# First round of a graph kernel: additions between the two comparisons of a group, block numbers loaded word by word

## The chip, the cores and the metric

The kernel runs on one core of a Trainium2 chip. The metric is the device time of one execution in microseconds (us); lower is better. Engines are named as the profile names them: PE is TensorE, PEld its weight loads, DVE VectorE, ACT ScalarE, POOL GpSimd, SP SyncE.

## The reference, cut to what matters

There are 12500 nodes with 64 features and 400000 edges `(src, dst)`, sorted by `dst`. Three rounds each sum rows of a node table over the edges that end in a node (`segment_sum`); between them stand small products, a relu and two layer norms.

```python
def _L0_gnn_ref(x, src, dst, W_fc, b_fc, W_res, b_res):
    agg = jax.ops.segment_sum(x[src], dst, num_segments=n)
    deg = jax.ops.segment_sum(jnp.ones_like(dst, dtype=x.dtype), dst, num_segments=n)
    mean = agg / jnp.maximum(deg, 1.0)[:, None]
    h = jnp.concatenate([x, mean], axis=-1) @ W_fc + b_fc
    h = jax.nn.relu(h)
    return h + x @ W_res + b_res
...
def _general_conv(x, edge_attr, src, dst, Wm, bm, We, be, Ws, bs):
    msg = x[src] @ Wm + bm + edge_attr @ We + be
    agg = jax.ops.segment_sum(msg, dst, num_segments=x.shape[0])
    return agg + x @ Ws + bs
...
x = _layernorm(x + _L0_gnn_ref(x, src, dst, ...), axis=-1)
x = _layernorm(x + _L1_gnn_ref(x, edge_index, edge_attr_64, ...), axis=-1)
```

## The kernel before

**The first round**, which the change touches, fills about 260 to 1485 us of the span. It goes over 72 blocks of 128 destination nodes, two per turn of a loop (`j` is 0 or 1); the work on one block is called a half here. For each block it builds a 128 x 12544 matrix of edge counts and multiplies it with the node table. The edges are cut into steps of 128. For a step VectorE writes two comparisons into a ring of 16 places (`hot_c`): the high one, which marks the source block and the place in a window of `wd` destination nodes, and the low one, which marks the source lane (both by `pairs`, whose instruction is line 816). TensorE multiplies the one with the other (L1149), ScalarE copies the counts out of PSUM (L1418), SyncE stores them, and TensorE multiplies the counts of the block before with the table (the dense product, L1126, in 16 pieces of 6 or 7 matmuls).

**Widths.** Windows are 1 node wide in blocks 0 to 7, 2 nodes in blocks 8 to 29, 4 nodes in blocks 30 to 71. So a half has 128 steps at width one (after the first two blocks, which have several steps for a window), 64 at width two and 32 at width four. The comparisons come in groups: 8 steps (`many`) at widths one and two, 4 at width four. A half thus has 16, 8 and 8 groups. Width two holds 22 halves, 486 to 860 us; width four 42 halves, from 858 us.

**The handshake.** Before a group VectorE waits on `stepped`, which lets it start when TensorE has done the steps of the group two before (8-step groups; 4-step groups have four places in the ring). The low comparison of a group raises `made`, on which TensorE waits before the steps of the group.

**Edges that are not counted in the matrix** are gathered: GpSimd issues 7 indirect DMAs for a half (L1288), VectorE marks their destination lanes (`hot_g`, L797), TensorE multiplies them at the end of the half (L1118, 21 matmuls) into 7 sums. VectorE then adds, in the next half, with one instruction each:

- part 0: the reduction of the dense product into `part_d` (L853), after waits on `b_used` and `gsum`, and before it the load of 7 block numbers, packed in two words, into registers (`load_blocks`, whose instruction is L471)
- part 1: `part_d` to its block of `acc` (L859)
- parts 2 to 8: the 7 sums, each to a block of `acc` that a loaded number names (L865); each waits on `s_add`, which the addition before it raises
- part 9: a semaphore (`gred`).

Part `n` stands at window 10 + 2n of the half. At width one each such window begins a group; at widths two and four every second one does (windows 12, 16, 20, 24, 28), and the others (10, 14, 18, 22, 26) lie within one. Where a group begins, the order is: wait on `stepped`, high comparison, low comparison, then the part.

The order on each engine is the order in the code; nothing reorders it.

## Time and profile before

| what | value |
|---|---|
| median of 3 runs (lowest, highest) | 3532.28 us (3532.06, 3535.52) |
| the profiled execution | 3533.11 us, span 3531.3 us |
| PE busy | 3093.6 us, 88% |
| DVE busy | 2388.2 us, 68% |
| POOL busy | 2120.9 us, 60% |
| ACT busy | 1585.1 us, 45% |
| L816, comparisons of the first round | x1384, 911.7 us busy |
| L865, additions of gathered sums | x504, 110.0 us busy, 69.0 us idle before them |
| L853, reductions of the first round | x72 |

The profile is one execution. A group of instructions is given with its count, busy time and the time its engine sat idle in front of it. A busy PE counts modelled ends of pipelined matmuls, so its rate is better read from the distance between starts.

### The profile page before, as it was taken

The numbers are of one execution on the slowest core, as the hardware profiler recorded it, in microseconds if no ns is written. First come the engines' busy times: TensorE is split into PE (matmuls) and PEld (weight loads), VectorE is DVE, ScalarE is ACT, GpSimd is POOL, SyncE is SP. The second block draws the span as 40 slices with busy tenths as digits, with TensorE's granted clock in tenths as the row PEclk, the third lists the DMA queues.
The fourth block names the chain that finished last, engine by engine and source line by source line (L and its number), as shares of the span: only waits on it lengthen the run. The fifth ranks groups of instructions, "written<-read, shape, count | busy, mean of one in ns | idle before, by whom it ended". The sixth has DMA issues, their size and how long they took to land.

```text
span 3531.3 us, 114817 instructions
## 1 busy us (share of the span) xinstructions
PE 3093.6 (88%) x38568; PEld 2874.1 (81%) x38568; DVE 2388.2 (68%) x6286; ACT 1585.1 (45%) x2164; POOL 2120.9 (60%) x2436
## 2 busy tenths in 40 slices
PE   0128999999999999899999979999999889999995
PEld 0127988888888888788888879999999789999995
DVE  8679998888888888799999673333333433333335
ACT  0122677778999999789999550000000400000000
POOL 5771345455666666544444257777777777777774
PEclk9859999999999999999999879999999999999998
DMA  3521455556666666678888439999999499999995
GB/s 87 144 19 44 163 196 208 202 211 229 239 244 243 244 242 243 233 229 253 253 253 252 119 139 384 393 396 381 400 384 384 172 363 394 393 387 398 386 388 222
DMA packets 234014, 928.09 MB, mean 263 GB/s; under 512 B 46723, under 2 KB 146193, under 8 KB 178030
## 3 DMA queue, kind: packets, MB, share of 16 engines
q1 hardware_dynamic: 182405, 844.73, 63.8%
q0 software_dynamic: 51392, 80.97, 7.9%
q10 hardware_dynamic: 154, 1.60, 0.2%
q8 instruction: 34, 0.56, 0.1%
q14 instruction: 29, 0.24, 0.0%
HBM read 676.56 MB, written 250.56 MB: 263 GB/s over the span
## 4 chain that ended last, share of the span: by engine, by line
PE 40%; POOL 19%; issue 17%; DVE 14%; DMA 5%; DVEq 5%; ACT 1%; ACTq 0%; POOLq 0%; SPq 0%
PE ps L1126 27%; POOL msg L1288 13%; PE ps L1149 8%; DVE union L816 5%; DMA msg<-y_tab,idx 3%; POOL abuf L1230 3%; DVE union L931 3%; PE ps L1118 3%; DVE abuf L944 3%; DVEq L944 2%; DVEq L471 2%; POOL union L1230 1%; PE ps L1086 1%; DMA abuf<-in_x_dram 1%; PE ps L1205 1%
## 5 line engine op out<-in xcount | busy, mean ns | idle before, releaser
L1288 POOL DMA_INDIRECT msg<-y_tab,idx x1512 | 1611.3, 1066 | 922.2 <-issue 469.6
L1126 PE MATMUL ps<-union,abuf 128*128 128x192 bf16 x14112 | 1206.4, 248 | 14.9 <-DVEq L787 10.2
L1126 PEld LDWEIGHTS ps<-union,abuf 128*128 128x128 f16 x14112 | 1173.6, 99 | 17.9 <-issue 10.6
L1418 ACT ACTIVATE abuf<-ps 128x784 f16<-128x784 f32 x1152 | 949.1, 824 | 261.4 <-PE ps L1149 236.6
L816 DVE TENSOR_TENSOR union<-lane,union 128x1568 f16<-128x1568 f16 (+1 forms) x1384 | 911.7, 710 | 8.5 <-PE ps L1149 4.6
L1126 PE MATMUL ps<-early,abuf 128*128 128x195 bf16 x7154 | 809.3, 249 | 0.0
L1126 PEld LDWEIGHTS ps<-early,abuf 128*128 128x128 f16 x7154 | 641.9, 99 | 92.1
L1149 PE MATMUL ps<-union 128*128 128x98 f16 (+2 forms) x4192 | 661.8, 287 | 56.7 <-DVE union L816 55.5
L1394 ACT ACTIVATE idx<-src_g 128x7 int32 (+1 forms) x216 | 44.4, 205 | 1257.1 <-PE ps L1118 1237.9
L808 DVE TENSOR_TENSOR acc<-acc,ps 128x64 f32 (+1 forms) x1015 | 225.0, 222 | 412.4 <-DVE acc L808 239.3
L1196 PE MATMUL ps<-union 128*64 128x128 f32 x7280 | 458.7, 278 | 24.0 <-ACT union L1440 19.6
L1196 PEld LDWEIGHTS ps<-union 128*64 128x64 f32 x7280 | 395.5, 137 | 87.4 <-DVE abuf L944 74.3
L1440 ACT ACTIVATE union<-union 128x1280 f32<-128x1280 f16 x364 | 443.5, 1268 | 35.8 <-DVE union L931 35.3
L1149 PEld LDWEIGHTS ps<-union 128*128 128x128 f16 x4192 | 353.7, 108 | 98.5 <-issue 59.3
L1308 POOL TENSOR_TENSOR rel_e<-early,base_e 128x10 f16 x728 | 226.1, 330 | 247.4 <-DVE union L931 244.5
L931 DVE TENSOR_TENSOR union<-lane,rel_e 128x640 f16<-128x640 f16 x728 | 352.2, 484 | 4.4 <-POOL rel_e L1308 1.4
L895 DVE TENSOR_REDUCE part_d<-ps 128x64 f32<-128x192 f32 x144 | 51.6, 358 | 353.1 <-PE ps L1126 353.1
L794 DVE TENSOR_SCALAR hot_g<-lane,codes 128x128 f16<-128x128 f16 x1008 | 184.2, 269 | 63.9 <-DVE acc L808 62.2
L1118 PE MATMUL ps<-msg,hot_g 128*128 128x64 bf16 (+1 forms) x4536 | 181.7, 195 | 45.8 <-DMA msg<-y_tab,idx 45.3
L944 DVE TENSOR_TENSOR abuf<-abuf,ps 128x128 f32 x728 | 204.9, 281 | 15.8 <-issue 7.2
L1118 PEld LDWEIGHTS ps<-msg,hot_g 128*128 128x128 f16 x4536 | 169.1, 99 | 54.4 <-DMA msg<-y_tab,idx 53.8
L865 DVE TENSOR_TENSOR acc<-acc,ps 128x65 f32 x504 | 110.0, 218 | 69.0 <-DVE acc L865 53.8
(229 smaller groups left out, 1342.2 us busy)
## 6 DMA issues: line engine op xcount, KB each, us to landing
abuf<-a_dram SPq DMA_DIRECT2D x288, 1568.0 KB
a_dram<-abuf SPq DMA_DIRECT2D x72, 3136.0 KB
union<-in_edge_attr_dram SPq DMA_DIRECT2D x728, 160.0 KB, 3.1
msg<-y_tab,idx POOLq DMA_INDIRECT x1512
y_tab<-union SPq DMA_DIRECT2D x28, 336.0 KB, 2.2
abuf<-in_x_dram SPq DMA_DIRECT2D x28, 224.0 KB, 3.5
y_tab<-early SPq DMA_DIRECT2D x7, 682.5 KB, 5.2
out_dram<-union SPq DMA_DIRECT2D x2, 800.0 KB, 3.5
```

Source lines behind the costliest of these rows:

```text
L808: V.tensor_tensor(to, to, tile_ps(r, j, k).unsqueeze(1), ALU.add).then_inc(s_add[r], 1)
L816: return V.tensor_tensor(to.rearrange("p s (c u) -> p s c u", u=2), lanes.unsqueeze(1).to_broadcast([P, n, width // 2, 2]), codes[:, which ...
L931: marks = V.tensor_tensor(mark_e[:, h, :, :].rearrange("p j (c u) -> p j c u", u=2), lane16[:, 0:P].rearrange("p (c u) -> p c u", u=2).uns ...
L944: V.tensor_tensor(to, to, ps[:, b, 0:P], ALU.add).then_inc(e_add, 1)
L1118: last = nc.tensor.matmul(tile_ps(r, j, k), hot_g[:, s, :], msg[:, s, c * width_of[r]:(c + 1) * width_of[r]], start=c == 0, stop=c == 2)
L1126: last = nc.tensor.matmul(ps[:, bank, 0:3 * width_of[r]], abuf[:, buffer, hi * P:(hi + 1) * P], ycols[r][:, hi, :], start=hi == 0, stop=hi ...
L1149: nc.tensor.matmul(ps[:, w % 4, 0:WIN].rearrange("p (h d) -> p h d", d=WD)[:, :, d0:d0 + wd], hot_c[:, n, WIN:WIN + P], hot_c[:, n, 0:HIS ...
L1196: last = nc.tensor.matmul(ps[half:half + D, h, 0:P], feats[:, h, j * D:(j + 1) * D], hot_e[:, h, j, :], start=j < 2, stop=j >= EG - 2)
L1288: pool.indirect_dma_start(msg[:, s, 0:3 * width_of[r]], None, y_tab[r], bass.IndirectOffsetOnAxis(ap=idx[:, s:s + 1], axis=0)).then_inc(ga ...
L1308: nc.gpsimd.tensor_tensor(rel_e[:, h, :, :], flat(dst_e[:, bass.ds(grp[h], 1), :]).unsqueeze(2) .to_broadcast([P, EG, 2]), base_e[:, bass. ...
L1418: A.activation(abuf[:, j, :].rearrange("p (h w d) -> p w h d", w=WPB, d=WD) [:, w:w + 2, :, :], ps[:, w % 4:w % 4 + 2, 0:WIN].rearrange("p ...
L1440: A.activation(hot_e[:, h:h + 2, :, :], mark_e[:, h:h + 2, :, :], ACT.Copy)\
```

## The change

`load_blocks` is called twice with 4 numbers (one word) instead of once with 8 (two words): at window 6 and at window 8 of the half, no longer behind the wait on `b_used` at window 10. The parts are put into a function `beside`, which is called behind the high comparison and ahead of the low one where a window begins a group. Where it does not, the part stands where it stood. Each part has the same waits as before.

```diff
+                        gathers, words = b0 < 2 * GI, []
+                        def beside(window, it, j, i):
+                            part, odd = divmod(window - 10, 2)
+                            if odd or part < -2 or part > (G + 2 if gathers else 1):
+                                return
+                            before = it * (2 * (G + 1)) + (1 + j * (G + 1))
+                            if part < 0:
+                                if gathers:
+                                    words.extend(load_blocks((it * 2 + j) * (GW // 4) + (part + 2), 4))
+                            elif part == 0:
+                                dve.wait_ge(b_used[j], it + (1 + j))
+                                if gathers:
+                                    dve.wait_ge(gsum[0][1 - j], it + (1 + j))
+                                V.tensor_reduce(part_d[:, j, :], ...).then_inc(b_red[j], 1)
...
+                                dve.wait_ge(s_add[0], before + (k + 1))
+                                if k < G:
+                                    to = flat(acc[:, bass.ds(words[-GW + k], 1), :])
+                                    V.tensor_tensor(to, to, tile_ps(0, 1 - j, k), ALU.add).then_inc(s_add[0], 1)
...
                                         dve.wait_ge(stepped, i * pair + (q + e0 + many - HB + 1))
                                         pairs(hot_c[:, n:n + many, 0:HIS * wd], twice_h, s, HIS * wd)
+                                    if q in upto[j]:
+                                        beside(upto[j].index(q), it, j, i)
+                                    if q % many == 0:
                                         pairs(hot_c[:, n:n + many, WIN:WIN + P], twice_l, s, P).then_inc(made, many // HB)
-                                    if q not in upto[j]:
-                                        continue
...
-                                            bs = load_blocks((it * 2 + j) * (GW // 4), GW)
```

On VectorE at width two, around the loads and the reduction. ISA and REGISTER_ALU rows set registers; 128x8x196 is a high comparison, 128x8x128 a low one. Before:

```order
L816 ISA [waits stepped]
L816 TENSOR_TENSOR union<-lane,union 128x8x196
L816 ISA
L816 TENSOR_TENSOR union<-lane,union 128x8x128
L471 ISA [waits b_used0]
L471 TENSOR_LOAD steps
L853 TENSOR_REDUCE part_d<-ps 128x65 [waits gsum0_1]
```

And now:

```order
L471 ISA
L471 TENSOR_LOAD steps
L868 REGISTER_ALU
L816 ISA [waits stepped]
L816 TENSOR_TENSOR union<-lane,union 128x8x196
L471 ISA
L471 TENSOR_LOAD steps
L816 ISA
L816 TENSOR_TENSOR union<-lane,union 128x8x128
L844 TENSOR_REDUCE part_d<-ps 128x65 [waits gsum0_1,b_used0]
```

The first load stands a group earlier, the second between the two comparisons of the last group ahead of the reduction.

On VectorE at width two, one group with two additions (`acc<-acc,ps`). Before:

```order
L816 TENSOR_TENSOR union<-lane,union 128x8x196
L816 ISA
L816 TENSOR_TENSOR union<-lane,union 128x8x128
L862 REGISTER_ALU
L865 ISA [waits s_add0]
L865 TENSOR_TENSOR acc<-acc,ps 128x65
L862 REGISTER_ALU
L865 REGISTER_ALU [waits s_add0]
L865 ISA
L865 TENSOR_TENSOR acc<-acc,ps 128x65
```

And now:

```order
L816 TENSOR_TENSOR union<-lane,union 128x8x196
L852 REGISTER_ALU
L855 ISA [waits s_add0]
L855 TENSOR_TENSOR acc<-acc,ps 128x65
L816 ISA
L816 TENSOR_TENSOR union<-lane,union 128x8x128
L852 REGISTER_ALU
L855 REGISTER_ALU [waits s_add0]
L855 ISA
L855 TENSOR_TENSOR acc<-acc,ps 128x65
```

The two additions no longer follow each other: the low comparison stands between them.

On VectorE at width one, the load. Before:

```order
L816 ISA [waits stepped]
L816 TENSOR_TENSOR union<-lane,union 128x8x98
L816 ISA
L816 TENSOR_TENSOR union<-lane,union 128x8x128
L471 ISA [waits b_used0]
L471 TENSOR_LOAD steps
L853 TENSOR_REDUCE part_d<-ps 128x65 [waits gsum0_1]
```

And now:

```order
L816 TENSOR_TENSOR union<-lane,union 128x8x98
L471 ISA
L471 TENSOR_LOAD steps
L816 ISA
L816 TENSOR_TENSOR union<-lane,union 128x8x128
L868 REGISTER_ALU
L816 ISA [waits stepped]
L816 TENSOR_TENSOR union<-lane,union 128x8x98
L471 ISA
L471 TENSOR_LOAD steps
L816 ISA
L816 TENSOR_TENSOR union<-lane,union 128x8x128
```

Both loads stand between the comparisons of a group here. The order on PE, ACT, POOL and SP is the same in both kernels.

## Rows read from the trace of the kernel before

**Rows 1.** Widths two, four: busy us PE, PEld, DVE, ACT, POOL; clock, DMA share, GB/s
```profile
486.00:860.00 374.00, 340.48 (x4062) 315.22 (x4060) 335.29 (x576) 292.87 (x377) 191.22 (x154) 1.00 0.55 210
860.00:1000.00 140.00, 137.56 (x1426) 115.58 (x1425) 124.03 (x252) 125.89 (x161) 93.74 (x68) 1.00 0.65 249
```

**Rows 2.** Waits at width two, 488 to 860 us: total us, times, longest
```profile
PEld ps L1149 <- issue: 58.7, 111, 0.6
PE ps L1149 <- DVE union L816: 33.5, 111, 0.4
DVE acc L865 <- DVE acc L865: 18.5, 66, 0.3
DVE part_d L853 <- issue: 10.5, 22, 0.5
```

**Rows 3.** Timeline of DVE at width two: start, us, instruction, idle before it
```profile
506.44 1.58 DVE L816 TENSOR_TENSOR union<-lane,union 128x1568 f16<-128x1568 f16 x2 [0.16 <-PE ps L1149]
508.51 0.36 DVE L853 TENSOR_REDUCE part_d<-ps 128x65 f32<-128x195 f32 x1 [0.49 <-issue]
508.79 1.57 DVE L816 TENSOR_TENSOR union<-lane,union 128x1568 f16<-128x1568 f16 x2
...
510.97 1.58 DVE L816 TENSOR_TENSOR union<-lane,union 128x1568 f16<-128x1568 f16 x2
512.46 0.21 DVE L865 TENSOR_TENSOR acc<-acc,ps 128x65 f32 x1
512.98 0.22 DVE L865 TENSOR_TENSOR acc<-acc,ps 128x65 f32 x1 [0.30 <-DVE acc L865]
513.22 1.58 DVE L816 TENSOR_TENSOR union<-lane,union 128x1568 f16<-128x1568 f16 x2
```

**Rows 4.** Timeline of PE in the same half
```profile
504.24 0.84 PE L1118 MATMUL ps<-msg,hot_g 128*128 128x65 bf16 x21
504.92 0.51 PE L1149 MATMUL ps<-union 128*128 128x196 f16 x4
...
506.64 0.50 PE L1149 MATMUL ps<-union 128*128 128x196 f16 x4
...
510.49 0.51 PE L1149 MATMUL ps<-union 128*128 128x196 f16 x4 [0.27 <-DVE union L816]
...
521.85 0.51 PE L1149 MATMUL ps<-union 128*128 128x196 f16 x4
```

**Rows 5.** Timeline of DVE at width one
```profile
411.97 0.21 DVE L865 TENSOR_TENSOR acc<-acc,ps 128x65 f32 x1
412.10 1.15 DVE L816 TENSOR_TENSOR union<-lane,union 128x784 f16<-128x784 f16 x2
```

**Rows 6.** Loads of block numbers (L471), four stretches: ns shortest/median/longest; the last: one word each
```profile
L471 DVEq TENSOR_LOAD <-steps x6: 1796/1843/1912, 364.7 to 471.3; - x6
L471 DVEq TENSOR_LOAD <-steps x23: 525/1722/1775, 489.8 to 859.4; - x23
L471 DVEq TENSOR_LOAD <-steps x42: 524/528/533, 873.8 to 1471.2; - x42
L471 DVEq TENSOR_LOAD <-steps x183: 299/305/526, 1501.6 to 1975.9; - x183
```

**Rows 7.** Timeline at width four, two of POOL's gathers and one pair of DVE
```profile
1009.74 1.31 DVE L816 TENSOR_TENSOR union<-lane,union 128x1568 f16<-128x1568 f16 x2
1009.92 1.62 POOL L1288 DMA_INDIRECT msg<-y_tab,idx  x1 [0.30 <-issue]
...
1019.04 0.94 POOL L1288 DMA_INDIRECT msg<-y_tab,idx  x1 [0.30 <-issue]
```

**Rows 8.** Wait for gathers at width four, 860 to 1485 us: total us, times, longest
```profile
PEld ps L1118 <- DMA msg<-y_tab,idx: 12.2, 21, 1.5
```

**Rows 9.** Timeline of POOL at width two: the first gather of the half
```profile
505.76 1.34 POOL L1288 DMA_INDIRECT msg<-y_tab,idx  x1 [7.06 <-ACT idx L1394]
```

**Rows 10.** Chain of waits at width four: start, us; from the last gather's start until it landed
```profile
1019.04 2.58 DMA msg<-y_tab,idx
```

34 lines of the change are left out of this document (10 added, 24 removed).

## The prediction

> **What bounds the kernel now.** First the busy time by stretch: the change touches only the first round, so the question is what ends last at each width. At width four PE is busy 137.6 of 140 us and DVE 124.0; at width two PE has 340.5 of 374 and DVE 335.3. The granted clock is 1.00 in both [rows 1]. So width four is TensorE's, and width two is shared: neither engine is full, which means that they wait for each other.
>
> The waits at width two say where. PE waits 111 times for comparisons, five times in each of 22 halves; its matmuls show 33.5 us and its weight loads 58.7 us [rows 2]. DVE waits 66 times for its own last addition, 18.5 us, and 22 times with nothing to wait for but its queue in front of the reduction, 10.5 us [rows 2].
>
> The timeline of one half shows the mechanism. A pair of comparisons that begins at 510.97 makes room for an addition at 512.46, 1.49 us later. The next addition needs the semaphore of the first, sits idle for 0.30 us and starts at 512.98, and the next pair starts at 513.22: 0.76 us for two additions, 2.25 us for the group [rows 3]. TensorE, undisturbed, starts at 504.92 and is two of its pieces of 4 steps (with their dense matmuls) further at 506.64: 1.72 us for a group of 8 steps [rows 4]. So while there are additions VectorE needs 2.25 us for what TensorE does in 1.72, and ring places are only two groups. From 504.92 to 521.85 the half takes 16.93 us. TensorE's own work in it is 8 x 1.715, plus 0.17 for the two pieces with a seventh dense matmul, plus 0.68 for the gathered product (504.24 to 504.92): 14.57 us [rows 4]. The difference, 2.36 us, times 22 is 52 us, and agrees with the 58.7 us of the weight loads: this is the most that width two can give.
>
> **The change part by part.**
>
> *Additions apart.* Where an addition follows and precedes comparisons and its semaphore has long come, as at width one, it costs the distance from 411.97 to 412.10: 0.13 us, since it overlaps with both neighbours [rows 5]. With a comparison between any two additions I take that price for both: the group costs 1.49 + 0.26 = 1.75 us instead of 2.25. The bounds are 0.13 and the 0.38 of each of two dependent additions (0.76 / 2) [rows 3, 5]; I take the low one because the waited-for addition is then at least one low comparison old.
>
> *What it costs in `made`.* The low comparison now ends behind an addition, so a group takes 1.57 + 0.13 = 1.70 us from its start to `made`. I walk through the half with three distances. The high comparison starts at the earliest 1.52 us after TensorE starts the group two before (504.92 to 506.44); TensorE starts 0.13 us after the pair ends (508.79 + 1.57 = 510.36, to 510.49); TensorE needs 1.715 us for a group [rows 3, 4]. Zero is 504.92. Group 2 starts at 1.52 as before, the reduction 1.49 later at 3.01 and group 3 another 0.28 later, at 3.29 (before: 3.87). Its steps start at 3.29 + 1.70 + 0.13 = 5.12, and TensorE is free for them at 5.15. Group 4: 5.04, steps at 6.87 (free at 6.87). Then VectorE starts every 1.75 us: 6.79, 8.54, 10.29, and TensorE starts at 8.62, 10.37 and, since group 7 has no addition, 12.09. From there 1.715 + 0.17 + 0.68 gives 14.65 us for the half. The waits are almost gone, and the bound is TensorE again.
>
> *Loads.* Before, the load of two words stood bare in front of the reduction: 0.49 us of idle at width two [rows 3]. It is in front of the reduction no more. The load at window 6 stands behind a finished pair, ahead of a wait for TensorE at 1.52, and is hidden by that wait. The load at window 8 stands between the comparisons of group 2. What one word costs there no row shows. The ends are 0.305 us, the median of single words in the later edge stage, and 1.91 us, the longest load of two words at width one; in this very stage two words took 1.72 us, but 0.53 at width four [rows 6]. I take half of 1.72, 0.86 us. About 0.9 us of the high comparison cover it (it has 1568 of the pair's 2592 elements, so 0.6 of 1.49 us), and with the register work ahead of it the low comparison is some 0.2 us late. That moves groups 3 to 7 by 0.2: 14.85 us for the half; I take 14.8. So 16.93 - 14.8 = 2.1 us, times 22 = **46 us** gained. With 0.305 us for the word it is 50 us.
>
> *Width one* (6 halves): each part already stood between two groups, so there was no idle to win. One load of 1.84 us behind a pair of 1.15 goes, of which some 1.0 was bare [rows 5, 6]; two loads behind a high comparison of about 0.55, half of a pair, come. At 0.86 each, and with register work, they stick out by about 0.5 each: nothing gained, nothing lost. Ends: -6 us (both hidden) and, at 1.84 us a word, 2 x 1.5 - 1.0 = 2.0 us a half, +12. The blocks before 362 us have the same order in two halves more: 0, at most 4 us lost.
>
> *Width four* (42 halves): the additions win the same 0.5 us a group on VectorE, and it is waste, since TensorE is full. What is late there is the gather: TensorE waits in every second half for the last of 7 gathers, 21 times, 12.2 us in all [rows 8]. A gather takes 0.94 us at its shortest. The one at 1009.92 lasts until 1011.54, 0.49 us past the end (1011.05) of the pair that was started just before it [rows 7], and the next begins 0.30 later, 1.92 us after the first. A group with two additions is 1.31 - 0.09 + 0.76 = 1.98 us here at most, so gathers seem to go in step with the groups, and such a group becomes 1.22 + 0.26 = 1.48. Some five gathers in step win 0.4 us each, more than the wait. I take **10 us**. Ends: 0 and 12.2 us.
>
> The Trainium skill (SBUF — State Buffer, section Who interferes with whom) says that a VectorE instruction with two SBUF inputs blocks a GpSimd instruction that reads SBUF until it ends. The trace agrees as far as it goes: the gather that began 0.18 us after a pair lasts 1.62 us, the shortest 0.94 [rows 7]. Were it a slowdown by share of time instead, denser comparisons would make gathers slower, and the 10 us would not come.
>
> *Clock, stores, evacuations*: at width two the DMA share would rise from 0.55 towards the 0.65 of width four, ACT's load from 292.9 / 374 to the level of 125.9 / 140 [rows 1]. Both are met there at the full clock, so I price them at nothing.
>
> Sum: 46 + 0 + 10 = 56 us from the profiled execution's 3533.1: 3477. The median of the runs lies 0.8 us below that execution; I say **3477 us**.
>
> **The rivals.**
>
> *The word costs as much as two did.* At 1.72 us the low comparison of group 2 comes 1.1 us late; the half becomes 15.7, 22 x 1.25 = 27 us. Width one loses 12, width four gives 10: 3508 us. For it: at widths one and two, where VectorE waits for TensorE, the typical load took 1.7 to 1.9 us [rows 6], and the second load keeps a place just behind such a wait. Against: the edge stage's words at 0.305.
>
> *The gathers become the bound.* The first one starts 1.52 us after the gathered product of the half before (504.24 to 505.76), six distances later the last one starts, and it lands 2.58 us on [rows 4, 9, 10]. In step with groups of 1.75 us that is 4.1 + 10.5 = 14.6 us: just the half. If they fall into a beat of 2.0 us, as at width four now, it is 4.1 + 12 = 16.1 us a half: 22 x 0.8 = 18 us and nothing at width four, 3515 us.
>
> *The gap stays.* The Trainium skill (VectorE: DVE Perf Modes, section The DRAIN you can't avoid) says that chained instructions cost the same with or without a semaphore after each, because the pipe drains anyway. As a mechanism here: the 0.76 us of two additions would be their own price wherever they stand, `made` would come later by it, and the load would be as long between the comparisons as it was bare. Then nothing changes: 3530 us. Against it stand 0.13 us at width one and 0.76 / 2 = 0.38 at width two for the same instruction [rows 3, 5].
>
> *Slower.* An addition between a high and a low comparison may lose its overlap on both sides and hold the low one, as a dependent addition does: (0.76 - 0.26) = 0.5 us more, now once a group ahead of `made`. Let x be that extra. Width two loses 4x in 22 halves (88x) of its 46; width one, where nothing was won, has 9 such additions in 6 halves (54x); width four has at least 1.6 us of room in a half (DVE's 16 idle us of 140 [rows 1]) and loses nothing at this x, but also wins nothing if gathers stay. At x = 0.5: -46 + 44 + 27 = +25, less 10 if the gathers still gain: +15, so 3548 us. It decides from x = 0.39, where 142x is 56. Against it: addition and comparison overlap today in both orders.
>
> **How the numbers follow.** Forecast 0.60, own range 3465 to 3492. Full price of a word 0.14; gathers bound 0.08; gap stays 0.05; slower 0.08; a gain beyond the forecast, with width one at its full speed, 0.05. A measurement tells about 0.2% (7 us) from no change. Faster by more: 0.60 + 0.14 + 0.08 + 0.05 = 0.87. Same 0.05. Slower 0.08. The range goes from 3463 (46 + 4 + 12 + 6 with nothing lost) to 3512, which takes in the full price of the word and nearly the gathers.
>
> **What would show it.** In the profile after, at width two: no idle time between additions; two pieces of TensorE every 1.72 us through the half; halves of 14.8 us; the 111 waits for L816 at under 15 us. The length of the single load between comparisons: 0.3, 0.9 or 1.7 us. At width four the waits for gathers gone, halves at 14.4, and the reduction waiting longer for the gathered product. Width one unchanged at 21 us a half. Wrong it would be if a low comparison starts more than 0.3 us behind the addition ahead of it, or gathers lie 1.9 us apart.

## The result and the profile after

The changed kernel takes **3624.8 us** (median of 4 runs, 3621.8 to 3627.1) against 3533.9 us for the kernel before: ratio 1.0256, 95% interval 1.024 to 1.0272. The forecast was 3477 us with a range from 3463 to 3512. It was wrong in sign: a gain was forecast and a loss came. One run of a later kernel (e6, 3758.5 us at a granted clock of 0.83) was in a slower state and is left out of every number.

The profiled execution took 3621.8 us, its span is 3620.0 us, 88.7 us longer than before. It splits at one instruction, the last `hot_g` of the first round, the last start in this row of the view of one line (duration ns, first and last start):

```profile
L797 DVE TENSOR_TENSOR hot_g<-code_g,lane x72: 1081/1084/1093, 260.3 to 1457.0; 128x896 f16<-128x896 f16 x72
```

```profile
L797 DVE TENSOR_TENSOR hot_g<-code_g,lane x72: 1082/1084/1093, 260.2 to 1525.1; 128x896 f16<-128x896 f16 x72
```

The first is the kernel before, the second the one after: 68.1 us are lost in the first round, and 20.6 us behind it. In what follows "last `hot_g`" is this number; it measures the first round alone. The first `hot_g` starts between 259.5 and 262.0 us in these kernels, so a difference of 2 us in it says nothing.

The table of stretches after, to be held against [rows 1]:

```profile
486.00:860.00 374.00, 290.62 (x3368) 280.15 (x3366) 264.50 (x476) 242.65 (x313) 191.92 (x128) 0.88 0.46 175
860.00:1000.00 140.00, 121.42 (x1330) 109.70 (x1330) 110.62 (x216) 106.18 (x137) 77.26 (x56) 0.93 0.54 204
1000.00:1480.00 480.00, 479.34 (x5012) 406.04 (x5011) 424.51 (x867) 441.25 (x565) 292.84 (x234) 1.00 0.66 247
```

From 486 to 860 us TensorE now does 3368 matmuls instead of 4062, every engine is less busy, and the granted clock is 0.88. From 1000 us on TensorE is full and the clock 1.00. So something stops all engines at width two. The waits between 488 and 1000 us name it:

```profile
ACT abuf L1423 <- PE ps L1154: 150.5, 61, 12.0
DVE union L816 <- PE ps L1154: 131.3, 32, 12.3
PEld ps L1123 <- DMA msg<-y_tab,idx: 104.3, 12, 10.6
PE ps L1154 <- DVE union L816: 0.3, 1, 0.3
```

The 111 waits of TensorE for comparisons [rows 2] are one of 0.3 us: the change did what it was for. In their place TensorE waits 12 times for the gathers (L1123 is the gathered product, L1118 before), up to 10.6 us, and ScalarE and VectorE wait for TensorE.

The timelines of VectorE, GpSimd, SyncE and TensorE around the first of these stops. In VectorE's, a row of 1568 elements with x2 is a high and a low comparison, one behind the other, and x4 is two such pairs:

```profile
498.41 0.22 DVE L855 TENSOR_TENSOR acc<-acc,ps 128x65 f32 x1
498.54 1.57 DVE L816 TENSOR_TENSOR union<-lane,union 128x1568 f16<-128x1568 f16 x2
500.03 1.09 DVE L797 TENSOR_TENSOR hot_g<-code_g,lane 128x896 f16<-128x896 f16 x1
501.03 3.06 DVE L816 TENSOR_TENSOR union<-lane,union 128x1568 f16<-128x1568 f16 x4
```

```profile
495.38 1.45 POOL L1293 DMA_INDIRECT msg<-y_tab,idx  x1 [0.30 <-issue]
497.14 1.44 POOL L1293 DMA_INDIRECT msg<-y_tab,idx  x1 [0.31 <-issue]
498.88 6.03 POOL L1293 DMA_INDIRECT msg<-y_tab,idx  x1 [0.30 <-issue]
505.21 0.94 POOL L1293 DMA_INDIRECT msg<-y_tab,idx  x1 [0.30 <-issue]
```

```profile
503.01 0.37 SPq L1554 DMA_DIRECT2D a_dram<-abuf  x1
```

```profile
511.04 1.33 PE L1123 MATMUL ps<-msg,hot_g 128*128 128x65 bf16 x21 [8.75 <-DMA msg<-y_tab,idx]
```

Read them together. The seventh gather of the half starts at 498.88, 0.34 us into the high comparison of the last group. It lasts 6.03 us; its neighbour behind it 0.94. It ends at 504.91, and VectorE's run without an idle moment ends at 501.03 + 3.06 = 504.09: 0.82 us earlier. Meanwhile SyncE has issued the half's 3.2 MB store at 503.01. TensorE gets the gathered rows only at 511.04. The 6 us gather comes 11 times, at 498.88, 539.55, 580.55 and so on to 908.30, in every second half: after a stop the next seven gathers run at 1.25 us apart on an idle VectorE, so the next half is not touched. At 662.53 it is the sixth gather of its half instead of the seventh: there GpSimd pauses for 1.76 us between its first and its second gather, where 0.30 us is usual. Each trace has such a pause of 1.7 to 1.8 us between 600 and 660 us, the kernel before too, and it is behind most of what the table below calls "once" or "all but one".

The stop costs TensorE its clock as well:

```profile
504.00:505.00 1.00, 0.00 (x0) 0.00 (x0) 0.09 (x1) 0.00 (x0) 0.91 (x1) 1.00 1.05 439
506.00:508.00 2.00, 0.00 (x0) 0.00 (x0) 0.00 (x0) 0.00 (x0) 1.39 (x3) 0.50 1.00 401
512.00:514.00 2.00, 2.00 (x19) 1.85 (x17) 0.00 (x0) 0.82 (x1) 1.33 (x2) 0.50 0.49 125
516.00:518.00 2.00, 2.00 (x24) 1.97 (x23) 1.32 (x3) 1.54 (x2) 0.00 (x0) 0.94 0.03 8
```

TensorE is idle from about 502.3 us; in the row from 506 on the granted clock is 0.50, the 1.2 GHz level, and it is still 0.50 for the first pieces behind the stop. Rows of the timeline of TensorE:

```profile
512.19 0.84 PE L1154 MATMUL ps<-union 128*128 128x196 f16 x4
...
513.81 0.86 PE L1154 MATMUL ps<-union 128*128 128x196 f16 x4
...
515.44 0.86 PE L1154 MATMUL ps<-union 128*128 128x196 f16 x4
...
516.69 0.50 PE L1154 MATMUL ps<-union 128*128 128x196 f16 x4
```

From the gathered product (511.04) to the first piece it is 1.15 us instead of 0.69, and the pieces are 1.62, 1.63 and 1.25 us apart instead of the 0.86 of the pieces from 516.69 on: 2.4 us lost in all. The row of 506 to 508 also shows the DMA engines full, at 401 GB/s; at that rate the 3.2 MB of the store take 8 us (an estimate from this row), from 503.4 to about 511.4, and TensorE gets the gathered rows at about that time.

The halves between the stops are as forecast: from one `hot_g` (525.85) to the next (540.70) 14.85 us; the forecast said 14.85 by its walk. The long halves take 25.8 to 26.8 us. So width two took 450.2 us instead of 371.8 (+78.4); blocks 30 to 71 took 589.6 instead of 599.9 (-10.3); width one and the blocks before it are unchanged (block 8 begins at 485.3 in both).

### The profile page after: what moved, and what is told of

The parts are those of the page before. It is cut to its first block, busy times and chain, and to the rows that moved or that the text cites. A ratio compares the mean times of both kernels' runs of the same rounds, so it can differ in the third digit from the quotient of the medians.

```text
span 3620.0 us, 115031 instructions
## 1 busy us (share of the span) xinstructions
PE 3125.4 (86%) x38568; PEld 2913.9 (80%) x38568; DVE 2370.9 (65%) x6286; ACT 1588.8 (44%) x2164; POOL 2123.0 (59%) x2436
## 4 chain that ended last, share of the span: by engine, by line
PE 45%; POOL 18%; issue 15%; DVE 10%; DMA 8%; DVEq 4%; ACT 1%; POOLq 0%; ACTq 0%; SPq 0%
PE ps L1131 30%; POOL msg L1293 12%; PE ps L1154 10%; DMA msg<-y_tab,idx 6%; POOL abuf L1235 3%; DVE union L936 3%; PE ps L1123 3%; DVE abuf L949 2%; DVE union L816 2%; DVEq L949 2%; DVEq L471 1%; POOL union L1235 1%; PE ps L1210 1%; PE ps L1091 1%; DMA abuf<-in_x_dram 1%
## 5 line engine op out<-in xcount | busy, mean ns | idle before, releaser
L1131 PEld LDWEIGHTS ps<-union,abuf 128*128 128x128 f16 x14112 | 1173.1, 99 | 16.7 <-issue 10.6
L816 DVE TENSOR_TENSOR union<-lane,union 128x1568 f16<-128x1568 f16 (+1 forms) x1384 | 939.1, 711 | 142.5 <-PE ps L1154 132.3
L1131 PE MATMUL ps<-early,abuf 128*128 128x195 bf16 x7154 | 820.2, 251 | 0.0
L1131 PEld LDWEIGHTS ps<-early,abuf 128*128 128x128 f16 x7154 | 650.6, 100 | 93.9
L1154 PE MATMUL ps<-union 128*128 128x98 f16 (+2 forms) x4192 | 671.5, 290 | 20.5 <-DVE union L816 16.4
L1154 PEld LDWEIGHTS ps<-union 128*128 128x128 f16 x4192 | 361.5, 110 | 50.7 <-DVE union L816 29.3
L1123 PE MATMUL ps<-msg,hot_g 128*128 128x64 bf16 (+1 forms) x4536 | 186.8, 197 | 140.4 <-DMA msg<-y_tab,idx 140.4
L1123 PEld LDWEIGHTS ps<-msg,hot_g 128*128 128x128 f16 x4536 | 174.4, 100 | 147.4 <-DMA msg<-y_tab,idx 147.0
```

The source lines that it names most:

```text
L816: return V.tensor_tensor(to.rearrange("p s (c u) -> p s c u", u=2), lanes.unsqueeze(1).to_broadcast([P, n, width // 2, 2]), codes[:, which ...
L1123: last = nc.tensor.matmul(tile_ps(r, j, k), hot_g[:, s, :], msg[:, s, c * width_of[r]:(c + 1) * width_of[r]], start=c == 0, stop=c == 2)
L1131: last = nc.tensor.matmul(ps[:, bank, 0:3 * width_of[r]], abuf[:, buffer, hi * P:(hi + 1) * P], ycols[r][:, hi, :], start=hi == 0, stop=hi ...
L1154: nc.tensor.matmul(ps[:, w % 4, 0:WIN].rearrange("p (h d) -> p h d", d=WD)[:, :, d0:d0 + wd], hot_c[:, n, WIN:WIN + P], hot_c[:, n, 0:HIS ...
```

## The experiments

The long gathers are read from GpSimd's timeline between 486 and 1480 us, the last `hot_g` as above. The runs of most kernels fall into two heaps 16 to 23 us apart, of which e12 tells. Where both are given, each is the median of its heap; elsewhere the time is the median of all runs, and one run of e3 (3492) and two of e4 (3553, 3554) stand in the lower heap. The long halves of the changed kernel and its like are given by their median. Of the two kernels that the table leaves out, e7 and e8, their sections tell.

| kernel | long gathers, us each | long halves at width two, us | last `hot_g` | time, us (lowest, highest) |
|---|---|---|---|---|
| before | none | 16.9 (all) | 1457.0 | 3533 (3527, 3556) |
| changed | 11 of 6.03 | 26.1 | 1525.1 | 3625 (3622, 3628) |
| e1 additions alone | 1 of 5.29 | 15.1 (all but one) | 1423.5 | 3500 (3497, 3502) |
| e2 loads alone | none | 16.6 (all) | 1451.0 | 3532 and 3548 (3528, 3550) |
| e14 second word behind the low comparison | 11 of 6.03 | 26.2 | 1522.9 | 3619 (3618, 3620) |
| e13 last low comparison in two | 11 of 6.09 | 26.1 | 1528.2 | 3599 (3598, 3604) |
| e4 store waits for gathers | 11 of 6.03 | 20.5 to 21.3, once 22.6 | 1471.0 | 3570 (3553, 3572) |
| e10 memset behind first pair | 11 of 4.54 | 22.8, once 25.8 | 1492.0 | 3573 (3569, 3573) |
| e9 memset behind `hot_g` | 11 of 3.05 | 16.35, once 23.6 | 1427.3 | 3504 and 3526 (3503, 3527) |
| e3 memset ahead of `hot_g` | 20 of 2.05 | 15.3, once 16.8 | 1413.0 | 3512 (3492, 3513) |
| e5 small addition there | 20 of 2.06 | 15.3, once 16.6 | 1413.7 | 3512 (3509, 3515) |
| e6, e12 memset between last pair | none over 2.11 | 14.83 (all but one) | 1402.5 | 3482 and 3500 |
| e15 that, second word behind | none over 2.11 | 14.6 (all but one) | 1395.5 | 3476 and 3496 |

**e1: the additions alone.** The two words are loaded together, in front of the reduction, as before.

```diff
-                            if odd or part < -2 or part > (G + 2 if gathers else 1):
+                            if odd or part < 0 or part > (G + 2 if gathers else 1):
...
-                            if part < 0:
-                                if gathers:
-                                    words.extend(load_blocks((it * 2 + j) * (GW // 4) + (part + 2), 4))
-                            elif part == 0:
+                            if part == 0:
                                 dve.wait_ge(b_used[j], it + (1 + j))
                                 if gathers:
+                                    words.extend(load_blocks((it * 2 + j) * (GW // 4), GW))
```

> Only the additions stand between the two comparisons of a group; the two words of block numbers are loaded together again, in front of the reduction and behind its wait, which now stands between the comparisons of group 2. In the trace of the changed kernel (3620 us profiled) every second half at width two has a stall of about 11 us: the last gather of the half before lasts 6.03 us (498.88 to 504.91) instead of 0.94, its end 0.82 us behind the end of an unbroken run of VectorE's comparisons and hot_g, and its transfer then comes in behind the 3.2 MB store of the counts. Theory (lockout): the unbroken run is made by the additions going between the comparisons, so the stalls stay in this kernel, with 10 to 12 of the gathers of 6 us between 486 and 910 us: 3600 to 3640 us. Rival (places of the loads): the loads at windows 6 and 8 have moved VectorE's phase so that the gather falls badly; then the stalls go and 3480 to 3510 us come. Rival (transfers): denser halves make the stores denser and the gathers' transfers slow whatever VectorE does; then 3600 to 3640 too, but with gathers on GpSimd of 0.94 to 1.6 us.

Measured: 3499.7 us, ratio 0.9878 (0.9833 to 0.9923), one gather of 5.29 us (at 626.37) and one long half. The theory as written failed: additions between comparisons do not by themselves make the stops. What differs is seen at the reduction, in the timelines of VectorE and GpSimd of this kernel:

```profile
497.00 0.36 DVE L842 TENSOR_REDUCE part_d<-ps 128x65 f32<-128x195 f32 x1 [0.49 <-issue]
```

```profile
497.03 0.95 POOL L1291 DMA_INDIRECT msg<-y_tab,idx  x1 [0.30 <-issue]
498.29 0.94 POOL L1291 DMA_INDIRECT msg<-y_tab,idx  x1 [0.30 <-issue]
```

The double load still leaves VectorE idle for 0.49 us. The third gather starts with the reduction behind it, and it and the fourth take their shortest time. From the first gather's start to the seventh's it is 9.26 us (493.64 to 502.90), in the changed kernel 10.68 (488.20 to 498.88). So the seventh falls here into the group before the last, where an addition follows the high comparison; in the changed kernel it falls into the last group, which has none. It is so in every half of e1 but one: the seventh gather starts at least 0.68 us ahead of the last group's high comparison. The exception is the gather at 626.37. Behind GpSimd's pause it comes a group later, into the last low comparison.

**e2: the loads alone.** The reduction and the additions stand behind both comparisons.

```diff
+                                    window = upto[j].index(q) if q in upto[j] else None
+                                    if window is not None and window < 10:
+                                        beside(window, it, j, i)
                                     if q % many == 0:
                                         pairs(hot_c[:, n:n + many, WIN:WIN + P], twice_l, s, P).then_inc(made, many // HB)
+                                    if window is not None and window >= 10:
+                                        beside(window, it, j, i)
```

> Only the loads are changed: one word at window 6, one at window 8, the latter between the two comparisons; the reduction and all additions stand behind both comparisons as in the kernel before. Lockout theory: the idle time between dependent additions is back, each a gap of some 0.3 us in which a waiting gather can start, so there is no gather over 3.5 us and no stall; the 0.49 us of bare load go from each of 22 halves, less some 0.2 for the word between comparisons: 3520 to 3533 us. Rival (places of the loads): stalls as in the changed kernel, 3600 us or more.

Measured: ratio 1.000 (0.9973 to 1.0027), no long gather, last `hot_g` 6.0 us earlier than before, halves of 16.60 instead of 16.90. With the kernel before, e1 and the changed kernel the four combinations are there. The idle times between additions kept, or the one at the load kept: 0 or 1 stop. Both gone: 11. The timelines show a beat in place of them. In the changed kernel each gather waits for the end of the high comparison (1.45 us), the next starts 0.30 us later, and 1.45 + 0.30 is the 1.75 us of a group: from 493.63 to 498.88 exactly one gather goes with each group, always 0.34 us into its high comparison, and the seven reach the last group. Where the groups take 2.25 us, or one of them has an idle time, two gathers find room in a group now and then, and the seven are done more than a group sooner (9.55 us in the kernel before, from 505.76 [rows 9] to 515.31). There the seventh gather starts 1.7 to 3.3 us ahead of the last group's high comparison in all 22 halves, and in this kernel mostly 2.3 us ahead of it; in the changed kernel it (once the sixth) starts 0.34 us behind it in all 11 halves that end in a stop.

**e3: a memset ahead of `hot_g`.**

```diff
+        breath = sb("breath", [P, 16])
...
                                 if b0 < 2 * GI:
+                                    V.memset(breath[:, :], 0.0)
                                     g_mark(it, j)
```

> The changed kernel with one more VectorE instruction in each of the 72 halves of the first round, a memset of a 128x16 scratch tile just ahead of hot_g; it reads nothing from SBUF. Lockout theory: the gather that waits at the end of the half is let in there, so it ends about 1 to 2 us behind the memset instead of 5 us later; no gathers over 2.5 us, its transfer comes ahead of the store, all halves at width two 14.9 to 15.0 us, the stalls (12 x 11 us) are gone: 3475 to 3495 us. Rival (transfers): the late gather is a matter of the DMA queues and not of what VectorE executes; then nothing changes, 3615 to 3635 us. Rival (an idle gap is needed, not another kind of instruction): the gather still lasts 6 us and the time stays at 3615 to 3635, which this run alone does not tell from the one before except by the gather's length on GpSimd.

Measured: 3512 us (ratio 0.9898, 0.9844 to 0.9953), the long gathers at 2.05 us, no stops. VectorE and GpSimd in this kernel:

```profile
499.41 1.57 DVE L817 TENSOR_TENSOR union<-lane,union 128x1568 f16<-128x1568 f16 x2
500.92 1.07 DVE L798 TENSOR_TENSOR hot_g<-code_g,lane 128x896 f16<-128x896 f16 x1
500.93 0.07 DVE L864 MEMSET breath<- 128x16 f32 x1
```

```profile
499.75 2.05 POOL L1295 DMA_INDIRECT msg<-y_tab,idx  x1 [0.30 <-issue]
```

The gather starts 0.34 us into the high comparison, as in the changed kernel, and ends at 501.80, 0.82 us behind the end of the low comparison (499.41 + 1.57 = 500.98). 0.07 us of work for VectorE saves 4 us of GpSimd. That the transfers themselves are slow is refuted. So is a mere shift in time, since the gather starts at the same phase.

**e5: a small addition with two SBUF operands in the same place.** As e3 with `V.tensor_tensor(breath[:, :], lane16[:, 0:16], lane16[:, 0:16], ALU.add)`.

> As the kernel with the memset ahead of hot_g (profiled 3512 us, its last hot_g of the first round at 1413 us, no gather over 2.1 us), but the added instruction is an addition of 16 elements a partition that reads two operands from SBUF, at the same place and of about the same length. Theory (opening): a waiting gather is let in only where the next instruction of VectorE is not one with two SBUF operands; this one is, so the gathers of 6 us stay (10 or 11 of them), every second half at width two takes 25 to 27 us, the last hot_g of the first round stands at 1520 to 1530 us and the time at 3600 to 3630. Rival (phase): the memset helped only because it moved VectorE by some 0.1 us against the gathers, or because any short instruction lets a gather in; then this one helps as much: last hot_g at 1410 to 1420, 3490 to 3515 us.

Measured: 3512 us, gathers of 2.06 us, last `hot_g` 1413.7. The theory that it takes an instruction without two SBUF operands fell. The rival's second half holds: this short instruction lets the gather in too, at the end of the low comparison in front of it.

```profile
500.06 1.57 DVE L817 TENSOR_TENSOR union<-lane,union 128x1568 f16<-128x1568 f16 x2
501.54 0.16 DVE L864 TENSOR_TENSOR breath<-lane 128x16 f16<-128x16 f16 x1
501.63 1.08 DVE L798 TENSOR_TENSOR hot_g<-code_g,lane 128x896 f16<-128x896 f16 x1
```

```profile
500.39 2.07 POOL L1295 DMA_INDIRECT msg<-y_tab,idx  x1 [0.30 <-issue]
```

**e6, e9, e10: the memset at other places**, to set the length of the gather and see what each length costs. e6 puts it into part 9:

```diff
                                 else:
+                                    V.memset(breath[:, :], 0.0)
                                     dve.sem_inc(gred[0][1 - j], 1)
```

e9 puts it behind `g_mark(it, j)`, e10 behind the low comparison of the half's first group.

> The changed kernel with the memset of 128x16 in part 9, between the two comparisons of the last group of each half (at width two the only one of the groups 3 to 7 that has no addition there). Opening theory: the seventh gather, which starts 0.34 us into the high comparison of that group, is let in at the end of that comparison instead of at the end of the low one, so it takes 1.45 us instead of 2.05 with the memset ahead of hot_g and 6.03 without. Its data land 0.6 us earlier, and halves at width two take 14.85 to 15.1 us instead of 15.3: last hot_g of the first round at 1403 to 1410 us. The time is 3478 to 3487, or 20 us more if TensorE's clock falls at the start of the stretch between the rounds and not within it (the changed kernel and one loads-alone profile have that: 35.3 us for a stretch that takes 17.9 at the full clock). Rival (place does not matter, only that there is one memset a half): 15.3 us, last hot_g at 1413. Rival (the lock is passed only at hot_g): 6.03 us gathers again, 3620.

> The changed kernel with the memset of 128x16 just behind hot_g instead of just ahead of it. In the run with a small two-operand addition ahead of hot_g the gather was let in as well, at the same phase of its start (0.34 us into the high comparison), so the theory is now: any short instruction in VectorE's run lets it in, of whatever operands. Then the seventh gather ends 0.82 us behind hot_g: it takes 3.05 us (2.23 + 0.82), against 2.05 with the memset ahead of hot_g. It still ends about 1 us ahead of the issue of the store (4.1 us behind the gather's start in the changed kernel), so its transfer is not queued behind it: halves at width two about 1 us longer than 15.3, so 16.0 to 16.4 us, the last hot_g of the first round at 1428 to 1438 us, time 3500 to 3535 by the state of TensorE's clock between the rounds. Rival (only hot_g's length or place matters): 6.03 us gathers and 3620. Rival (phase): a shift of VectorE by 0.07 us behind hot_g changes nothing before the gather starts, so this theory too gives 6.03 us and 3620.

> The same memset one pair of comparisons later, behind the first group of the next half. Opening theory: the seventh gather takes 3.72 + 0.82 = 4.54 us, and ends 0.4 us behind the issue of the store. If being behind the store is what makes 6 us of the stall (as the run with SyncE's waits says: 20.5 to 21.3 us instead of 25.8 to 26.1 for the long half), the long halves appear again here, at 24 to 26 us, though the gather is only 1.5 us longer than with the memset behind hot_g: last hot_g at 1500 to 1525 us, time 3575 to 3620. Rival (the stall grows evenly with the gather's length): halves of 17.5 us, last hot_g at about 1460, time 3535 to 3560.

Measured: gathers of 1.45, 3.05 and 4.54 us, to the hundredth as foreseen. The last two:

```profile
501.15 3.05 POOL L1295 DMA_INDIRECT msg<-y_tab,idx  x1 [0.30 <-issue]
505.27 0.37 SPq L1556 DMA_DIRECT2D a_dram<-abuf  x1
505.76 0.85 PE L1125 MATMUL ps<-msg,hot_g 128*128 128x65 bf16 x21 [1.21 <-DMA msg<-y_tab,idx]
```

```profile
499.28 4.54 POOL L1296 DMA_INDIRECT msg<-y_tab,idx  x1 [0.30 <-issue]
503.40 0.37 SPq L1557 DMA_DIRECT2D a_dram<-abuf  x1
508.04 1.34 PE L1126 MATMUL ps<-msg,hot_g 128*128 128x65 bf16 x21 [5.35 <-DMA msg<-y_tab,idx]
```

With e9 the gather ends at 504.20, ahead of the store's issue, and TensorE waits 1.21 us. With e10 it ends at 503.82, 0.42 us behind the store's issue, and TensorE waits 5.35. The long half grows from 16.35 to 22.8 us for 1.5 us of gather. The rival of even growth (17.5 us) is out; my 24 to 26 us were too much. e6 took 3503 us (ratio 0.9887, 0.983 to 0.9944); its first round ends 54.5 us ahead of the kernel before.

**e4: the store waits for the half's gathers.**

```diff
                                 sp.wait_ge(evacd, i * (2 * WPB) + ((b0 + j + 1) * WPB + 3))
+                                sp.wait_ge(gathered[0][j], i * (16 * G) + (b0 // 2 + 1) * (16 * G))
```

> The changed kernel, but SyncE issues the store of a half's counts only when the gathers of its own half have landed. Nothing on VectorE changes. The stall of the changed kernel has two parts: the gather ends about 4 us late on GpSimd (504.91 where 0.94 us would have been 499.8), and its packets then run only at 509.8 to 510.6, while the store's run from 503.9. Theory: with the gathers ahead, their packets run about 1.5 us after GpSimd ends them, L1123 starts at about 507 instead of 511, and each of the 12 stalls falls from 11 to 6 or 7 us: 3560 to 3585 us, with the gathers of 6 us still there. Rival (the store costs nothing, the transfer is slow in itself): 3615 to 3635. Rival (slower): the store held back makes ScalarE and TensorE wait for its buffer in the halves without a stall, over 3640.

Measured: 3570 us, ratio 1.0082 (1.0059 to 1.0104). The 6.03 us gathers are all there, and the long halves take 21.1 us in the middle instead of 26.1: of the 11.2 us that a stop costs, some 5 come from the store being ahead of the gather. Here the store goes out 3 us behind the gather's end (648.89), not 1.9 us ahead of it:

```profile
642.86 6.03 POOL L1293 DMA_INDIRECT msg<-y_tab,idx  x1 [0.30 <-issue]
651.88 0.37 SPq L1555 DMA_DIRECT2D a_dram<-abuf  x1
```

**e7: e6 with e4's waits.**

> The kernel of the run before (memset in part 9) with SyncE's waits added: the store of a half's counts goes out only when the half's gathers have landed. If the last gather's transfer still trails the store now and then, this gives the rest: halves at width two at 14.85 and at width four at 14.42 throughout, last hot_g at 1398 to 1405 us. If the gathers are ahead of the store by themselves, nothing changes against the run before (within 2 us in the first round). Rival (slower): in halves without a stall the held store delays ScalarE's next block of counts; then the halves are longer than in the run before and the last hot_g is later than there.

Measured: 3503 us, last `hot_g` at 1404.5 instead of 1402.5, which is within what such numbers may differ by. Where no gather is late, the order of store and gather is worth nothing.

**e8: e1 with e6's memset.**

> The kernel with the additions alone between the comparisons (3499.7 us median; one stall at 626 us, where the first gather of a late chain started in the last low comparison ahead of hot_g; halves at 15.1 us; last hot_g at 1423.5 us) with the memset in part 9 as well. The memset stands ahead of that low comparison, so by the opening theory it helps only a gather that waits by then. If the stray stall is of the same kind (a seventh gather that slips into group 7), it goes: last hot_g at 1412 to 1414, 3489 us. If it stays, 1423 to 1425 and 3500. Against the changed kernel with the same memset this shows what the loads' new places are worth: 0.25 us in 22 halves and 5 us at width one, some 7 to 12 us, if the gathers do not eat it.

Measured: last `hot_g` at 1414.0 instead of 1423.5, no gather over 2.11 us (time 3498 to 3517). The stray stop of e1 is gone, but the memset did not end a wait there. The gather behind GpSimd's pause starts at 626.63, when the memset (626.47 to 626.54) is over, 0.09 us into the last low comparison; it takes 1.33 us and is let in at the end of that comparison, ahead of `hot_g`. In e1 the gather at 626.37, 0.2 us into the same comparison, was not. Why one was let in and the other not is open. Against e6 (1402.5) the new places of the loads are worth some 12 us.

**e13: the last low comparison cut in two**, each 4 steps, and nothing else.

```diff
+                                        a = 0
+                                        if wd == 2 and q + many == upto[j][WPB]:
+                                            a = many // 2
+                                            pairs(hot_c[:, n:n + a, WIN:WIN + P], twice_l, bass.ds(i * pair + (q + s0), a), P)
+                                            s = bass.ds(i * pair + (q + s0 + a), many - a)
-                                        pairs(hot_c[:, n:n + many, WIN:WIN + P], twice_l, s, P).then_inc(made, many // HB)
+                                        pairs(hot_c[:, n + a:n + many, WIN:WIN + P], twice_l, s, P).then_inc(made, many // HB)
```

> The changed kernel with the low comparison of the last group of each half at width two cut into two instructions of 4 steps each (about 0.35 us each; nothing else is added). If being short is what lets a gather in, a comparison of 0.35 us may do it: then the seventh gather, which starts 0.34 us into the high comparison, ends 0.82 us behind the end of that one or of the first half (1.45 or about 1.8 us), the stalls are gone, the last hot_g of the first round stands at 1402 to 1412 us, and the time is 3480 to 3487 or 3499 to 3510 by the heap of the clock. If it takes a foreign or a much shorter instruction, the gather lasts 6.1 us again, every second half takes 26 us, and the time is 3620 to 3630. I give the first 0.4 and the second 0.6, since at width four low comparisons of 0.42 us stand in unbroken runs and some gathers were let in at them and some not.

Measured: 11 gathers of 6.09 us. A comparison of 0.42 us lets no gather in here, and an addition of 0.16 us did in e5. But this does not make it a matter of length: at width four of the changed kernel the same comparison of 0.42 us stands between a high one and `hot_g`, and the gather that starts in the high one is let in ahead of it, 41 times of 41, as here:

```profile
1003.50 1.31 DVE L816 TENSOR_TENSOR union<-lane,union 128x1568 f16<-128x1568 f16 x2
```

```profile
1003.95 1.34 POOL L1293 DMA_INDIRECT msg<-y_tab,idx  x1 [0.30 <-issue]
```

Such gathers start some 0.45 us into the high comparison, those that are shut out 0.34 us. Whether the moment of the start decides was not tried; no run moved it within the last high comparison at width two.

**e14: the second word behind the low comparison.**

```diff
                                     window = upto[j].index(q) if q in upto[j] else None
-                                    if q in upto[j]:
-                                        beside(upto[j].index(q), it, j, i)
+                                    if window is not None and window != 8:
+                                        beside(window, it, j, i)
                                     if q % many == 0:
                                         pairs(hot_c[:, n:n + many, WIN:WIN + P], twice_l, s, P).then_inc(made, many // HB)
+                                    if window == 8:
+                                        beside(window, it, j, i)
```

> The changed kernel with the second word of block numbers loaded behind the low comparison of its group instead of ahead of it. Reading (place of the load): behind the low comparison the load is partly bare, VectorE idles some 0.3 us ahead of the next instruction, an early gather is let in there and the chain of seven is 0.5 us or more shorter, so the seventh falls into the sixth group with an addition behind it: no or at most a few gathers of 6 us, halves at width two of 14.9 to 15.2 us, last hot_g at 1405 to 1425, time 3485 to 3525. Rival (the additions make the stalls whatever the load does, and the kernel with the additions alone escaped by its bare double load of 0.5 us only): 8 or more gathers of 6 us, 3600 to 3630.

Measured: the rival. 11 gathers of 6.03 us, 3619 us. The expected idle time does not come. A single word hides wholly behind the low comparison:

```profile
529.40 1.58 DVE L816 TENSOR_TENSOR union<-lane,union 128x1568 f16<-128x1568 f16 x2 [0.34 <-PE ps L1157]
530.89 0.35 DVE L844 TENSOR_REDUCE part_d<-ps 128x65 f32<-128x195 f32 x1
```

No idle time in front of the reduction, so no opening either. It also gives what the word costs between the comparisons: halves of 14.59 us here, 14.84 there.

**e11, e12: the changed kernel and e6 once more.**

> The changed kernel once more, with more runs, beside the next one on the same chip. Of its 91 us over the kernel before, 68 are in the first round (last hot_g at 1525.1 against 1457.0 us) and 20.6 behind it, where TensorE's clock stands at 0.50 through a stretch of pure TensorE work between the rounds (35.8 us of waiting for it instead of 17.9). The runs of the kernel before fall in two heaps, near 3532 (21 of 30) and near 3552. Theory: which heap a run falls in is chance with a share that differs from kernel to kernel; the changed kernel has been in the upper heap 4 times of 4. Expected: 3620 to 3628 in most runs, with at most some at 3600 to 3608, and ratio 1.024 to 1.027 where before is at 3532.

> The kernel with the memset in part 9 (last hot_g at 1402.5 us, 54.5 ahead of the kernel before; 3503 us) once more, with more runs. If its runs can fall into the lower heap as well, some stand at 3480 to 3486, where the first round's gain is seen undiminished; if the changed order in front of the stretch always puts it into the upper one, all stand at 3500 to 3507.

Measured: 3625.8 us, ratio 1.0256 (1.0236 to 1.0276), all five runs from 3621.7 to 3628.3; and for e12 two runs at 3481.6 and 3483.2, four from 3498.9 to 3502.2. (Of the 30 earlier runs of the kernel before, 23 and not 21 were near 3532.)

The distance of the two heaps lies in one place, a stretch of about 150 matmuls without other work between the rounds. The kernel before and the changed one there, same columns as [rows 1]:

```profile
1981.00:1997.00 16.00, 16.00 (x146) 16.00 (x145) 0.15 (x1) 5.33 (x9) 0.00 (x0) 1.00 0.01 2
```

```profile
2057.00:2089.00 32.00, 32.00 (x152) 32.00 (x151) 0.00 (x0) 5.37 (x9) 0.00 (x0) 0.50 0.00 1
```

The same work takes 16 us at the full clock and 32 at the 1.2 GHz level. Behind it both kernels run at 0.50 for some 50 us, so what differs is when the clock falls: at the start of the stretch or behind it. By their times (one or two runs of each were profiled) the kernel before fell early in 11 of 65 runs, the changed kernel in 9 of 9, e1 in 0 of 4, e7 in 4 of 4. e13 has the first round of the changed kernel, stops and all, and fell early in 0 of 4 (profiled, 2074.4 us from its last `hot_g` to the end; before 2074.3, changed 2094.9). So the stops in the first round do not bring it about. What does was not found.

**e15: e6's memset and e14's load together.**

> The changed kernel with two edits: the second word of block numbers is loaded behind the low comparison of its group, and the 128x16 memset stands in part 9 between the last two comparisons of a half. If both hold together: no gather over 2.2 us, halves at width two at 14.6 us, 0.22 us less than the memset alone (14.82), the last hot_g of the first round at 1396 to 1399 us instead of 1402.5, and the time 3476 to 3480 in the lower heap of the clock, 3494 to 3500 in the upper. Rival (gathers become the bound, since a chain of seven needs 6 x 1.75 + 2.6 + 1.5 = 14.6 us in step with VectorE): the halves stay at 14.8, nothing gained on the memset alone.

Measured: three runs from 3475.2 to 3477.5 us, three from 3495.1 to 3499.3; ratio 0.9875 (0.9848 to 0.9903) over both. Last `hot_g` at 1395.5, 61.5 us ahead of the kernel before. Width two in this kernel:

```profile
486.00:803.00 317.00, 315.61 (x3949) 309.80 (x3950) 310.46 (x585) 286.55 (x367) 208.51 (x153) 1.00 0.65 247
```

```profile
PEld ps L1128 <- DMA msg<-y_tab,idx: 1.5, 1, 1.5
```

TensorE is busy 315.6 of 317 us and waits once for a gather; the halves of 14.6 us are the 14.57 us that the prediction counted as TensorE's own work. This version beats both kernels.

## Why the prediction was wrong

**The bound at width two: right.** Weight loads and matmuls waited for VectorE, and the wait could be taken away: 111 waits became one of 0.3 us. In e6, where nothing else is in the way, halves take 14.83 us (forecast 14.8), and the first round ends 54.5 us sooner (forecast 56).

**An addition at 0.13 us: right.** In the changed kernel no idle time stands in front of an addition at width two, and starts are as walked: 498.41 to 498.54.

**The word: right in its effect, wrong in its length.** I took 0.86 us for a load between comparisons; at width two the loads of the changed kernel take 0.31 us in the median. The low comparison starts 0.17 us late, and the halves lose 0.25 us against e14. The rival at 1.72 us a word did not happen.

**Width one: right,** nothing gained or lost. Width four: 10.3 us gained against 10 forecast, and in the way described: halves that took 14.9 us now take 14.43.

**The gathers: the step that failed.** "Gathers seem to go in step with the groups" was read from width four and used only as a gain; at width two I costed a beat of 1.75 us and, as a rival, one of 2.0 (3515 us, chance 0.08). Neither has room for a gather that is shut out. What I took from the Trainium skill (SBUF — State Buffer, section Who interferes with whom), that a VectorE instruction with two SBUF inputs blocks a GpSimd instruction that reads SBUF until it ends, I used as the whole length of the wait. The trace shows a gather waiting through seven such instructions, 6.03 us; and by e5 the wait can end while such instructions still follow. The measurement decides: in these 11 halves the wait goes on, over six boundaries between such instructions, to an idle moment or a short instruction of VectorE.

What I should have asked of the rows: the 0.30 us idle times between additions and the 0.49 us in front of the reduction [rows 3] were counted as waste that nobody uses. They kept the gathers out of step with the groups. In the kernel before, the seventh gather starts 0.15 us into an addition behind such an idle time, two groups ahead of the last, and takes 0.94 us:

```profile
515.16 0.22 DVE L865 TENSOR_TENSOR acc<-acc,ps 128x65 f32 x1 [0.23 <-DVE acc L865]
```

```profile
515.31 0.94 POOL L1288 DMA_INDIRECT msg<-y_tab,idx  x1 [0.30 <-issue]
```

The last group with `hot_g` and two more groups behind it was a run of seven large instructions without an addition in the kernel before too; the change sends the seventh gather into it. My own walk had the six distances of 1.75 us, which put the seventh gather into the last group; I read off only when it lands. None of the signs that I had named for being wrong came: the gathers lay 1.75 us apart and not 1.9, and no low comparison came late behind an addition.

**Stores and clock at nothing: wrong once a gather was late.** They were priced by steady rows at width four, and in steady flow they do cost nothing (e7 agrees for the store). Behind a late gather they multiply it: some 5 us of each stop are the store's (e4), 2.4 us the work at half the clock.

**The end behind the first round: not in the forecast.** 20.6 us of the 88.7 are TensorE's clock between the rounds.

The sum: 11 stops of 11.24 us are +123.6; 22 halves that are 2.06 us shorter give -45.2 (together +78.4); width four -10.3; the clock between the rounds +20.6: +88.7 us.

A slip without effect: the terms named for the fast end of the range, 46 + 4 + 12 + 6 = 68 us, give 3465 and not 3463.

The rival on the slower side (an addition that loses its overlap) is refuted by the 0.13 us. The slower case that came was none of mine.

## What to carry to other kernels

An idle gap on one engine may be what keeps another engine out of step with it. Before closing gaps, look at what runs beside them and at its spread of durations: here gathers of 0.94, 1.24, 1.34 and 1.43 us in one half said that they were waiting for something. When a change makes an uninterrupted run longer or sends other work into one, look for the instruction of the other engine that can start in it; one tiny instruction in the right place (0.07 us) was worth 123 us of the first round here (1525.1 to 1402.5). And a late transfer must be priced with what is queued by then, not by itself.

## What the runs showed of the hardware

- A gather that had to wait ended 0.82 us behind the end of a VectorE instruction, in every kernel looked at: of a comparison in front of an addition (gather of 1.45 us), of a comparison or `hot_g` in front of a memset (1.45, 2.05, 3.05, 4.54 us by its place), of a comparison in front of a 0.16 us addition (2.06), or of the whole run (6.03).
- At some boundaries between two comparisons gathers are let in as well (at 509.14 in the kernel before, start 0.35 us into the high comparison, 1.43 us), at others never: with the start at 0.34 us, 11 of 11 at width two of the changed kernel. What tells these apart stays open. The length of the next instruction does not do it alone: 0.42 us did not let a gather in at width two (e13) and did 41 times of 41 at width four.
- In the stop shown, TensorE stopped at 502.3 us and its granted clock stood at 0.50 from the row of 506 us on; it resumed at 511.04, and the row of 516 to 518 shows 0.94.
